# Self attention in a decoder kernel: masks from the tokens' sums, and the sum of residual and beta, made by the pool engine

## The reference

```
Q, K, V = relu(x @ Wq + bq), relu(x @ Wk + bk), relu(x @ Wv + bv)     # 16 heads of 8 channels
scores = einsum('bqhd,bkhd->bhqk', Qh, Kh) / sqrt(8)
key_mask = sign(abs(sum(x, axis=-1)))
scores = where(key_mask == 0, NEG, scores); scores = where(tril == 0, NEG, scores)
attn = softmax(scores) * query_mask                                   # query_mask = key_mask
out = einsum('bhqk,bkhd->bqhd', attn, Vh) + x
return gamma * (out - mean) / sqrt(var + 1e-8) + beta
```

## Time and profile before

| what | value |
|---|---|
| three timed runs | 1497.22 us median (1489.43, 1497.22, 1498.69) |
| profiled execution | 1487.44 us, span 1485.7 us |
| busy over the span | PE 84%, PEld 68%, DVE 63%, ACT 49%, POOL 45% |
| mean granted clock of PE | 0.911 of full speed |
| transfers | 210.38 MB, mean 142 GB/s |
| self attention | sums of the first sequence at 30.1 us, offset of the last at 356.8 us |

### The profile page before, as it was taken

The page is one execution under the profiler, slowest core; times in us unless marked ns, Lnnn a source line. Parts: engine busy times, 40 slices in busy tenths (PEclk is TensorE's granted clock), DMA queues, the critical chain, the costliest instruction groups (busy, mean ns, idle before and its releaser), DMA issues. The chain is left out here.

```text
span 1485.7 us, 30220 instructions
## 1 busy us (share of the span) xinstructions
PE 1254.7 (84%) x9798; PEld 1016.1 (68%) x9798; DVE 941.3 (63%) x2822; ACT 728.1 (49%) x1527; POOL 662.0 (45%) x1138
## 2 busy tenths in 40 slices
PE   0599999988878799999997399992799999967998
PEld 0477776766656478888885288881677777756997
DVE  6479999987677678788873211113777888624554
ACT  0166666664454256565652255540355555544553
POOL 2044454463221156777776100005466666423555
PEclk9899999997786699999996599995899999987999
DMA  2677765424555344444430377754555555305775
GB/s 49 179 204 209 212 197 157 120 79 130 161 169 144 98 129 125 123 125 124 121 82 30 100 216 211 216 167 108 146 132 140 130 137 145 92 27 166 208 213 144
DMA packets 206817, 210.38 MB, mean 142 GB/s; under 512 B 46467, under 2 KB 159811, under 8 KB 206660
## 3 DMA queue, kind: packets, MB, share of 16 engines
q1 hardware_dynamic: 189780, 187.07, 46.8%
q10 hardware_dynamic: 12784, 12.98, 2.8%
q0 software_dynamic: 4096, 8.40, 1.9%
HBM read 121.84 MB, written 84.41 MB: 139 GB/s over the span
## 5 line engine op out<-in xcount | busy, mean ns | idle before, releaser
L1034 DVE TENSOR_REDUCE negmax<-scores 128x2 f32<-128x512 f32 (+1 forms) x576 | 391.5, 685 | 141.0 <-PE scores L645 89.4
L1180 POOL TENSOR_SCALAR_AFFINE_SELECT probs<-probs 128x256 f32<-128x256 f32 (+1 forms) x576 | 287.4, 504 | 272.8 <-ACT probs L873 268.3
L873 ACT ACTIVATE probs<-weights 128x512 f32<-128x512 f32 x448 | 266.0, 598 | 191.4 <-PE weights L686 139.3
L686 PE MATMUL weights<-queries,keys 104*128 104x256 f32 x768 | 165.1, 298 | 36.0 <-DMA queries<-maxrows 34.7
L648 PE MATMUL scores<-keys,queries 96*128 96x512 f32 x384 | 186.8, 487 | 1.1 <-issue 0.8
L686 PEld LDWEIGHTS weights<-queries,keys 104*128 104x128 f32 x768 | 129.4, 198 | 70.4 <-DMA queries<-maxrows 49.2
L873 ACT ACTIVATE probs<-weights,keybias 128x512 f32<-128x512 f32 x192 | 131.7, 688 | 89.1 <-PE weights L686 70.0
L1244 POOL DMA_INDIRECT out_room<-expert_rows,y_index x64 | 63.5, 993 | 193.5 <-POOLq L1468 180.9
L691 PEld LDWEIGHTS weights<-queries,keys 104*128 104x128 f32 x768 | 110.8, 195 | 17.8 <-ACT probs L873 6.1
L691 PE MATMUL weights<-queries,keys 104*128 104x128 f32 x768 | 110.7, 269 | 5.0 <-ACT probs L873 4.8
L650 PE MATMUL scores<-hide,ident_r 128*128 128x256 f32 x384 | 112.2, 292 | 0.0
(11 more groups left out here) (251 smaller groups left out, 2676.6 us busy)
## 6 DMA issues: line engine op xcount, KB each, us to landing
windows<-parts SPq DMA_DIRECT2D x192, 192.0 KB
queries<-windows SPq DMA_DIRECT2D x64, 384.0 KB
keys<-windows SPq DMA_DIRECT2D x192, 96.0 KB
hidden_room<-in_m_w SPq DMA_DIRECT2D x71, 256.0 KB, 2.8
out_room<-in_m_w SPq DMA_DIRECT2D x71, 256.0 KB, 3.2
routed_rows<-zeros SPq DMA_DIRECT2D x64, 256.0 KB, 3.1
windows<-parts ACTq DMA_DIRECT2D x64, 120.0 KB
xin<-routed_rows SPq DMA_DIRECT2D x39, 128.0 KB, 3.0
```

The source lines that it names most:

```text
L686: i = pe.matmul(bank[:, k * T:(k + 1) * T], keys[0:MREND, S4 * a + s, 0:P], queries[0:MREND, s, :], start=True, stop=True)
L873: act.activation(probs[:, n % RING], weight_banks[n % 2][:], ACT.Exp, scale=SCALE, **bias).then_inc(exp_done.sem, 1)
L1034: i = dve.tensor_reduce(most[:, t, s, heads], bank[:].rearrange("p (a k) -> p a k", k=P * (t + 1)), AX.X, ALU.max, negate=True)
L1180: pool.affine_select(out=block, in_=block, compare_op=ALU.is_ge, fill=0.0, base=0, pattern=[[0, heads], [1, P]], channel_multiplier=-1).th ...
```

## The change

The masks: DVE still makes `sums` and `gone`, but no longer the three masks. A new stage `pool_masks` on POOL, at f-22 with rank 1, waits for `gone` and for the transposes of unit g-2, and makes the three with the same operations. DVE waits for them before it makes `tok` (f-21), and before it overwrites `gone` it waits for the masks of unit g-1. The offset: DVE no longer makes it after the residual is added. A new stage `pool_offset`, at outputs+3 (f+34) with rank 1, waits for the residual's load and for the variance of the second norm of unit g-1, and makes it; DVE waits for it before L1099.

```
+        gone_ready, masks_ready, offset_ready = (signal(n, {"self": 1}) for n in ("gone_ready", "masks_ready", "offset_ready"))
@@ dve_prepare
                 step(dve.tensor_reduce(sums[:], x[:], AX.X, ALU.add))
                 settle(dve)
-                step(dve.tensor_scalar(gone[:], sums[:], 0.0, None, ALU.is_equal))
-                settle(dve)
-                if g >= 2:
-                    dve.wait_ge(transposed.sem, transposed.at(g - 2))
-                dve.tensor_scalar(keybias[:, seq], gone[:], -BIG, None, ALU.mult)
-                dve.tensor_scalar(keep2[g % 2][:], gone[:, :, None].to_broadcast([P, NT, 2]), -1.0, 1.0, ALU.mult, ALU.add)
-                step(dve.tensor_scalar(keeps[:, seq], gone[:], -1.0, 1.0, ALU.mult, ALU.add))
+                if g:
+                    dve.wait_ge(masks_ready.sem, masks_ready.at(g - 1))
+                dve.tensor_scalar(gone[:], sums[:], 0.0, None, ALU.is_equal).then_inc(gone_ready.sem, 1)
             yield from rest(1 if U.kind == "ffn" else 2)
 ...
             else:
-                settle(dve)
+                dve.wait_ge(masks_ready.sem, masks_ready.at(g))
                 for t in range(NT):
                     i = dve.tensor_scalar(tok[g % 2][:, t, :], x[:, t, :], keeps[:, seq, t:t + 1], None, ALU.mult)
@@ dve_outputs
-                dve.tensor_tensor(offset[:], resid[g % LANES][:], w["a_beta"][:, None, :].to_broadcast([P, NT, C]), ALU.add)
                 step(i)
 ...
                 dve.wait_ge(norm_rstd["post"].sem, norm_rstd["post"].at(g))
+                dve.wait_ge(offset_ready.sem, offset_ready.at(g))
                 dve.wait_ge(dve_step, centred)
@@ new on POOL
+        def pool_masks(pool, g):
+            seq = g % B
+            pool.wait_ge(gone_ready.sem, gone_ready.at(g))
+            if g >= 2:
+                pool.wait_ge(transposed.sem, transposed.at(g - 2))
+            pool.tensor_scalar(keybias[:, seq], gone[:], -BIG, None, ALU.mult)
+            pool.tensor_scalar(keep2[g % 2][:], gone[:, :, None].to_broadcast([P, NT, 2]), -1.0, 1.0, ALU.mult, ALU.add)
+            pool.tensor_scalar(keeps[:, seq], gone[:], -1.0, 1.0, ALU.mult, ALU.add).then_inc(masks_ready.sem, 1)
+            yield
+
+        def pool_offset(pool, g):
+            pool.wait_ge(resid_loaded.sem(g), resid_loaded.at(g))
+            if g:
+                pool.wait_ge(norm_var["last"].sem, norm_var["last"].at(g - 1))
+            pool.tensor_tensor(offset[:], resid[g % LANES][:], w["a_beta"][:, None, :].to_broadcast([P, NT, C]),
+                               ALU.add).then_inc(offset_ready.sem, 1)
+            yield
@@ pool_stages
-            return ((AT.split, 1, pool_copy_high), (U.attend, 0, pool_attend), (U.outputs + 5, 1, pool_post),
+            return ((AT.prepare + 1, 1, pool_masks), (AT.split, 1, pool_copy_high), (U.attend, 0, pool_attend),
+                    (U.outputs + 3, 1, pool_offset), (U.outputs + 5, 1, pool_post),
                     (U.outputs + 9, 1, pool_last))
```

## The result

Over 20 runs each, the changed kernel took 1485.51 us (median, 1480.01 to 1499.68) against 1492.62 us before (1485.04 to 1504.1). The ratio is 0.9955, with a 95% interval of 0.9937 to 0.9973: 6.7 us less, 4.0 to 9.4. The forecast was 7.2 us less. Timed again (e12), the same kernel gave 0.9966 (0.9941 to 0.9992). All ratios leave out three executions of the later runs that fell into a slow state (1533, 1626 and 3852 us).

A forecast was written before the change was run, and what follows sets the result against it. Bound: self attention's loop, 12.07 us of DVE's queue up to tok, then 5.41 of PE's, 17.52 per period. -4.75 - 2.55 - 0.7 + 0.8 = -7.2 us, from 1497.2 to 1490.0; gain range 2 to 12 us, overall 1478 to 1500.

The forecast's parts named there:

- the two levels: Three timed runs of the kernel before were said to lie near two levels some 9 us apart.
- What leaves DVE: Self stage, DVE's queue before tok: offset sum 0.34 us and masks 0.70 leave, 1.04 per period, taken as 0.85.
- one new hold: DVE held by a POOL instruction it collides with: some 0.2 to 0.4 us, only one new one certain per period.
- Typical periods: Eight self-stage periods: tok comes 0.85 us sooner, PE can use only its 0.62 wait before the maxima's transfer binds; gain 4.75 us.
- Late periods: Last three periods, from 249 us: PE waits 1.35 us for tok only, so the whole 0.85 counts; gain 2.55 us.
- Behind the last full period: After 289.46 us two more offset sums leave DVE's queue, where it has no idle time: gain 0.7 us.
- The start: Sequences 0 and 1: masks are on the path, and making them through POOL costs 0.4 us more each, 0.8 us lost.
- the transfer did not come along: Rival, self stage: the maxima's transfer lands earlier too, all 11 periods give 1.04 us; 12 us gained, 1485 us; chance 0.14.
- slip by what tok gains: Rival, self stage: the maxima's transfer slips, PE's wait for it grows from 0.58 to 1.2 us; no gain, 1497; chance 0.17.
- the first rival: Self stage: the maxima's transfer also lands earlier, so all 11 periods gain the full 1.04 us: 12 us; chance 0.14.
- The port: Rival, self stage: POOL's small instructions hold DVE, tok comes 0.95 us later per period; +13.5 us, 1511; chance 0.11.
- change of time behind 360 us: Stages after self attention: the prediction would be wrong if the time moved in a stage after 360 us.

The follow-up runs named there:

- e12: The changed kernel, unchanged, timed again against the kernel before: ratio 0.9966 (0.9941 to 0.9992).
- e4: The offset sum moved to POOL, the masks left on DVE, against the kernel before: every period 17.27 us, ratio 0.9986 (0.9959 to 1.0013).
- e8: The kernel before, with tok waiting for the step of its own masks, not DVE's latest step: periods 17.30 to 17.33 us, ratio 0.9972 (0.9947 to 0.9996).
- e5: The changed kernel with no stores of zeros issued between the windows and the maxima's transfer: periods 16.27 to 16.30 us, ratio to before 0.9897 (0.9867 to 0.9928).
- e7: The changed kernel with each mask and the offset sum made twice on POOL: late periods 16.49 in place of 16.29 us, ratio 0.9957 (0.9916 to 0.9998).
- e6: The kernel before, with the stores of zeros moved out of the maxima's transfer's way: periods 17.50 to 17.55 us, ratio 1.0004 (0.9978 to 1.003).

## Why the prediction was right, and where its sizes were off

The direction, the place and the mechanism held: one turn made of DVE's queue up to tok and PE's queue after it, the typical periods caught by the maxima's transfer, the late ones not, POOL's additions beside other work. The total was 7.2 against 6.7 us, but this closeness is partly luck. In the steady part the gain was 10.1 us, not 7.3, and some seems to be given back later. The range of 2 to 12 us was wider than the working: its own terms give at most 4.75 + 3 x 1.04 + 0.7 - 0.2 = 8.4 us, which the 10.8 us by unit 13 exceed. The forecast time of 1490.0 us missed the measured 1485.51 by 4.5, because the three runs that it started from have a median 4.6 us above that of all twenty; those fill the room from 1485 to 1504 us, and the two levels that the prediction saw in three runs are not there.

- **What leaves DVE**: taken as 0.85, measured 1.23. The offset: 0.34 us of place, 0.25 kept (e4), the rest lost to holds at maxparts, 0.28 in place of 0.19 us, as argued. The masks: 0.70 was measured from keybias, but DVE had also waited for gone to finish: from gone's start to the next maximum it was 0.9 us (209.84 to 210.74) and is 0.08. And 0.2 us came from the drain ahead of tok, which the working did not see (e8). The allowance of 0.2 us for one new hold was about twice the 0.09 us that came; the pair that adds the offset took 0.97 and takes 0.99.
- **Typical periods**: 0.59 us each was forecast (4.75 over eight), 0.86 came in six of them, though the transfer kept its place to 0.01 us. Here the wait for tok had been priced at its idle time. The idle time before an instruction is counted from the end of the one before, and PE overlaps them: the product at 212.83 lasts 0.50 us, but in the changed kernel the transposes start 0.34 us after it began, in the one before 1.12. The wait was worth the difference of the starts, 0.78 us. Of the rest, 0.05 lies in the products behind it (from the transposes to DVE's next wait 5.45 us before, 5.40 after).
- **Late periods**: 0.85 forecast, 1.23 measured, all of DVE's saving; the room of 1.35 us sufficed.
- **Behind the last full period**: 0.7 us forecast, 0.1 to 0.4 measured. From unit 11 to 13 it was 30.5 us in both profiles and is 30.4, 30.1 and 30.1. The prediction asked only whether DVE was idle there. PE is busy for 26.21 of the 27.04 us from 289.46 to unit 13 before, and for 26.20 of 26.93 after, so PE had almost no idle time to give.
- **The start**: 0.8 us forecast. The start shows tok waiting for POOL:

```profile
31.40 0.48 DVE L990 TENSOR_SCALAR tok<-xin,keeps 128x128 f32<-128x128 f32 x2 [0.67 <-POOL keeps L1198]
```

  tok starts at 31.40, not 31.10, and the second interval is 7.97 us, not 7.69: 0.3 us each, 0.6 in all. Unit 0 does not show it cleanly, because PE's clock differs there: it comes at 93.3 and 92.6 us before, at 92.2, 93.9 and 94.1 after, with a mean granted clock between 75 and 80 us of 0.60, 0.78, 0.86, 0.52 and 0.54. The first pair's 0.86 against 0.60 alone is worth some 1.3 us of PE's work in these 5 us, by estimate.
- **The rivals**: the transfer did not come along (10.94 against 10.95 us), nor did it slip by what tok gains. With e5's edit the self stage gains 11.8 us by unit 13, about the first rival's 12. The port cost about 0.1 us per period, and 0.2 more with its load doubled; the Trainium skill (SBUF — State Buffer, Who interferes with whom) is right that the two contend, and e7's rows show holds that end with the one POOL instruction that they meet.
- **After the stage**: the prediction counted no change of time behind 360 us and called such a change a sign of being wrong. The difference between 10.8 us at unit 13 and 6.7 or 5.1 at the end speaks for some, but where it arises stays open: each later section wanders by as much. From 300 to 510 us PE's clock is at its lower level for part of the time, with a mean granted clock of 0.79 and 0.79 before, 0.74, 0.78 and 0.76 after, and 0.80 in e5, which gives nothing back. That fits a loss through the clock, but no run tried it.

## What to carry to other kernels

When two engines are over 90% busy, find the turn that passes between them and split it into one engine's queue and the other's. What leaves the first part counts in full until the next thing in line, here a small transfer behind unrelated issues, ends last. Then look in that queue's order, because an edit that was worth nothing before (e6) may be worth the most afterwards (e5). A wait on an engine's own latest step also waits for whatever was issued just ahead of it: record the step that is needed. Value a removed wait by the distance of starts, not by the idle time shown.

## What the runs showed of the hardware

- A one-input instruction on 2 or 4 columns with immediates takes POOL 194 to 227 ns, and DVE's took 0.15 to 0.17 us alone. A sum of two 128x256 tiles from SBUF takes POOL 759 ns and DVE 412.
- keybias on DVE took 0.65 us while POOL was in a select, 0.17 alone: for such small instructions the hold was the larger part of the price. POOL's own took 0.23 in a typical period of the changed kernel, and 0.34 in e7 beside DVE's pair of the offset.
- A wait for DVE's latest step costs even where that step is on DVE itself: tok started 0.57 us behind the statistics with it and 0.39 without (e8).
- The start-to-start distance of two products on PE was 0.34 us where the first is listed with 0.50: 0.16 us of PE's wait behind such a product is hidden from the column of idle time.
- Executions of one kernel differ by up to 20 us over a thousand, while the section bound by one turn of instructions repeats within 1.2 us of 220. For a change of under 1% the section is the better measure, and the timed runs say what is left of it.
